# A graph network's attention rounds with edges on partitions instead of features

## Chip, cores and metric

One core of one Trainium2 chip. The metric is the device time of one launch in microseconds: 8402.46 us, median of three runs (8401.58 to 8409.89).

## What is computed

A stack of four graph layers over 3125 nodes and 103125 edges sorted by target node, with 64 features; each layer is added to its input and normalised. In the kernel they are seven rounds over the edges: one sum, two attention rounds, one relation-typed sum, three maxima. The attention rounds are these:

```
e = edge_attr @ we                                # 32 attributes per edge
ke = k[src] + e
score = sum(q[dst] * ke, axis=-1) / sqrt(64)
a = exp(score - segment_max(score, dst)[dst])
alpha = a / segment_sum(a, dst)[dst]
out = segment_sum(alpha[:, None] * (v[src] + e), dst) + x @ ws + bs
```

The products with `wk`, `wv` and `we` are taken out of the edges: an edge's row is [x of source (64), attributes (32), 1], 97 wide (`KA`); the query of a target node is projected onto those 97 columns beforehand, and the weighted row sums are multiplied by the value weights afterwards, per node.

## The kernel before, in words

Edges are padded to 202 chunks (`C`) of 512 (`EC`), each of four tiles (`TC`) of 128 edges. Every round is one software pipeline over its chunks, and each engine has its own instruction stream, written by `chunks(eng, steps, (lag, stage), ...)`: in step t it calls the stages in the order in which they are listed, each with chunk t minus its lag. Within an engine's stream nothing overtakes; between engines the stages wait for counters, and `wait(...)` names the counter and the chunk. Small buffers are rings: `U` = 4 slots for data that DMA brings, `V` = 2 for products on the chip and for the PSUM banks.

In an attention round a chunk goes this way. ACT copies the chunk's source indices (`indices`, L845); POOL gathers the source rows with one indirect DMA for each tile (L799), edges on partitions. SP fetches flags, one-hot tile, four windows of the query table and the attributes, which are stored with features on rows (`fetch`, from L713). PE turns the gathered rows so that features lie on partitions (`turn`, L948) and multiplies windows with one-hots to give each edge the query of its target (`query`, three bf16 parts for each tile, L973). DVE multiplies both (`product`, L1129). PE sums over features with a matrix of constants, which puts the score on all 97 rows (`score`, L981). DVE forms the running maximum (scan, L1152), two differences and the decay (L1156, L1159, L1161), ACT takes two exponentials (L870, L872), DVE weights the row (L1134) and sums it with a scan (L1095), whose factor drops to zero where a new target begins. PE turns the result back (`back`, L995), ACT copies and stores it (L864, L891). At the end of a round POOL gathers each node's last row (L809), and node-wise work follows.

The stage orders of the attention rounds are `(0, turn), (0, query), (1, score), (3, back)` on PE (L1001) and `(0, product), (2, accumulate), (1, maxima)` on DVE (L1165). The sum round also makes the one-hot tiles (L1102) that later rounds read. The relation round is a gather, a weighting on DVE (L1113), `turn`, scan and `back`.

## Time and profile before

| | |
|---|---|
| median of the runs | 8402.46 us |
| profiled execution, its own time | 8402.05 us |
| its span | 8400.2 us |
| busy: POOL, PE, DVE, ACT | 5613.3, 4720.2, 3677.3, 2039.9 us |
| gathers of source rows | 5656, 957 ns each |
| mean granted TensorE clock | 0.634 |
| DMA | 896.47 MB, mean 107 GB/s |

### The profile page before, as it was taken

To read this page: it belongs to the slowest core of one execution; us is meant where nothing else is said; L and a number is where in the kernel's file an instruction comes from. 1 tells how busy PE (TensorE), PEld (TensorE's weight loads), DVE (VectorE), ACT (ScalarE), POOL (GpSimd) and SP (SyncE) were. 2 spreads that over 40 slices of the span, in tenths; PEclk is the share of its full clock that TensorE was granted. 3 is DMA by queue.
4 is the path that set the end of the run, shared out by engine and by line. 5 is a ranking of instruction groups with operands and counts; after the bars stand their busy time and mean duration, and the time that the engine had idled before them with its cause. 6 is when DMAs were issued, how large, how long until landed. Compare 5 with 4: busy or idle time off the path is not lost.

```text
span 8400.2 us, 120802 instructions
## 1 busy us (share of the span) xinstructions
PE 4720.2 (56%) x23315; PEld 2797.9 (33%) x23315; DVE 3677.3 (44%) x5268; ACT 2039.9 (24%) x4886; POOL 5613.3 (67%) x5874
## 2 busy tenths in 40 slices
PE   2333347777766777776533333666646666566664
PEld 1222234444444444444222222333323333233332
DVE  5444459999967999994133332111111111111112
ACT  1111124444433444442111111111111111111111
POOL 6777756666645666662477775777767777677776
PEclk9999985555555555555555555555556656556555
DMA  4444446665645666662322223444434444444443
GB/s 127 121 127 122 124 92 129 129 130 129 130 96 115 130 130 130 130 130 45 95 59 59 59 59 74 112 112 112 112 88 112 112 112 112 89 108 112 112 112 86
DMA packets 1878056, 896.47 MB, mean 107 GB/s; under 512 B 1293716, under 2 KB 1754724, under 8 KB 1871588
## 3 DMA queue, kind: packets, MB, share of 16 engines
q1 hardware_dynamic: 769476, 429.40, 20.4%
q10 hardware_dynamic: 921120, 272.38, 14.1%
q0 software_dynamic: 187392, 193.93, 12.9%
q8 instruction: 25, 0.41, 0.0%
q14 instruction: 43, 0.35, 0.0%
HBM read 642.32 MB, written 252.51 MB: 107 GB/s over the span
## 4 chain that ended last, share of the span: by engine, by line
PE 23%; issue 18%; POOL 8%; DMA 3%; DVE 2%; ACT 1%; POOLq 0%; DVEq 0%; ACTq 0%
POOL rows L799 8%; PE ps L987 6%; PE ps L962 6%; PE ps L958 5%; DMA rows<-src_table,idx 2%; PE ps L995 2%; PE ps L512 1%; PE ps L563 1%; PE ps L948 1%; PE ps L505 0%; DVE rows L1113 0%; POOL agg L809 0%; DMA agg<-states_sum,last_i 0%; DMA states_sum<-hb 0%; DVE agg L618 0%
## 5 line engine op out<-in xcount | busy, mean ns | idle before, releaser
L799 POOL DMA_INDIRECT rows<-src_table,idx x5656 | 5411.7, 957 | 2553.3 <-issue 1590.2
L948 PE MATMUL ps<-ident,rows 128*64 128x128 f32 x3232 | 839.1, 414 | 1432.3 <-DVE rows L1113 672.6
L1095 DVE TENSOR_TENSOR_SCAN st<-pen,st,ps 128x512 f32<-128x512 f32 x300 | 383.8, 1279 | 2592.3 <-PE ps L987 2592.2
L958 PE MATMUL ps<-ident,rows 128*128 128x128 f32 x1212 | 563.0, 464 | 1173.8 <-issue 1025.6
L995 PEld LDWEIGHTS ps<-ident,st 64*128 64x128 f32 (+2 forms) x4444 | 689.5, 211 | 1269.6 <-issue 1226.5
L995 PE MATMUL ps<-ident,st 64*128 64x64 f32 (+2 forms) x4444 | 905.7, 355 | 242.1 <-issue 216.3
L948 PEld LDWEIGHTS ps<-ident,rows 128*64 128x64 f32 x3232 | 478.4, 164 | 1570.3 <-issue 1394.1
L981 PE MATMUL ps<-prod,eighth 97*97 97x512 f32 x808 | 681.9, 940 | 453.3 <-issue 430.5
L1095 DVE TENSOR_TENSOR_SCAN st<-xe,st,ps 64x512 f32<-64x512 fp8e4 x402 | 511.1, 1271 | 876.2 <-issue 457.7
L958 PEld LDWEIGHTS ps<-ident,rows 128*128 128x128 f32 x1212 | 219.2, 181 | 1430.2 <-issue 1268.4
L882 ACT ACTIVATE xe<-ps,b 128x512 f32<-128x512 f32 x303 | 208.2, 687 | 1916.9 <-PE ps L962 1916.9
L962 PE MATMUL ps<-sel,win 128*64 128x128 fp8e4 x7272 | 647.6, 313 | 0.0
L987 PE MATMUL ps<-xe,w 128*128 128x512 f32 x606 | 625.3, 1135 | 0.0
L856 ACT ACTIVATE pen<-sel 97x512 f32<-97x512 fp8e4 x404 | 254.4, 630 | 1474.1 <-DVE decay L1159 1474.1
L973 PEld LDWEIGHTS ps<-sel,win 128*97 128x97 bf16 x4848 | 586.3, 203 | 17.0
L973 PE MATMUL ps<-sel,win 128*97 128x128 fp8e4 x4848 | 586.4, 309 | 0.0
L1095 DVE TENSOR_TENSOR_SCAN st<-decay,st,msg 97x512 f32<-97x512 f32 x402 | 516.4, 1285 | 132.6 <-DVE msg L1134 131.7
L864 ACT ACTIVATE hb<-ps 128x256 f32<-128x256 f32 (+1 forms) x808 | 346.1, 428 | 762.8 <-PE ps L995 762.7
L1152 DVE TENSOR_TENSOR_SCAN runmax<-pen,runmax,ps 97x512 f32<-97x512 f32 x404 | 512.4, 1268 | 20.2 <-issue 2.2
L962 PEld LDWEIGHTS ps<-sel,win 128*64 128x64 bf16 x7272 | 357.3, 152 | 267.6 <-issue 263.5
L981 PEld LDWEIGHTS ps<-prod,eighth 97*97 97x97 f32 x808 | 142.1, 230 | 520.4 <-issue 505.5
L862 ACT ACTIVATE hb<-ps 128x512 f32<-128x512 f32 x303 | 180.9, 597 | 552.7 <-PE ps L995 520.8
(150 smaller groups left out, 4061.8 us busy)
## 6 DMA issues: line engine op xcount, KB each, us to landing
states_sum<-hb ACTq DMA_DIRECT2D x1010, 128.0 KB
win<-dst_table SPq DMA_DIRECT2D x1616, 72.8 KB
rows<-src_table,idx POOLq DMA_INDIRECT x5656, 2.4
states_att<-hb ACTq DMA_DIRECT2D x404, 194.0 KB
win<-dst_table ACTq DMA_DIRECT2D x1212, 48.0 KB
win<-dst_table SPq DMA_DIRECT2D x1212, 48.0 KB
dst_b<-in_dst_row SPq DMA_DIRECT2D x50, 1024.0 KB
sel<-onehots SPq DMA_DIRECT2D x303, 128.0 KB
```

The costliest lines, as they stand in the source:

```text
L799: pool.indirect_dma_start(rows[:, s, j * D:(j + 1) * D], None, srcs[q.r], bass.IndirectOffsetOnAxis(ap=idx[:, s, j:j + 1], axis=0))\
L856: nc.scalar.activation(pen[0:kw, s % V, :], sel[0:kw, s, EC:2 * EC], ACT.Copy, scale=BIG, bias=-BIG)\
L864: nc.scalar.activation(hb[:, s, 0:TC * kw], bank(BACK, s)[:, 0:TC * kw], ACT.Copy)\
L948: last = nc.tensor.matmul(bank(TURNED, s)[0:D, j * P:(j + 1) * P], rows[:, s, j * D:(j + 1) * D], ident[:, :], is_transpose=True, start=Tr ...
L958: nc.tensor.matmul(bank(TURNED, s)[:, at_j], rows[:, s, j * P:(j + 1) * P], ident[:, :], is_transpose=True, start=True, stop=False)
L962: last = nc.tensor.matmul(bank(TURNED, s)[h * D:h * D + D, at_j], win_pair(s, j, h)[:, i * D:(i + 1) * D], sel[:, s, h * EC + j * P:h * EC ...
L973: last = nc.tensor.matmul(bank(QUERY, s)[0:KA, j * P:(j + 1) * P], win_att(s, j)[:, i * KA:(i + 1) * KA], sel[:, s, j * P:(j + 1) * P], st ...
L981: nc.tensor.matmul(bank(SCORE, s)[0:KA, :], eighth[0:KA, 0:KA], prod[:, s % V, :], start=True, stop=True).then_inc(q.score_ready.sem, 1)
L987: nc.tensor.matmul(bank(QUERY, s), w2[:, q.r - 4, :], xe[:, s, :], start=True, stop=True).then_inc(q.lifted.sem, 1)
L995: last = nc.tensor.matmul(bank(BACK, s)[:, j * w:(j + 1) * w], st[0:w, s % V, j * P:(j + 1) * P], ident[0:w, 0:w], is_transpose=True, star ...
L1095: nc.vector.tensor_tensor_scan(st[0:w, s % V, :], d0, d1, init, op0, op1).then_inc(q.st_ready.sem, 1)
L1152: nc.vector.tensor_tensor_scan(m, pen[0:KA, s % V, :], bank(SCORE, s)[0:KA, :], before[:, 0:1], ALU.add, ALU.max).then_inc(q.max_ready.sem, 1)
```

## The change

All in the two attention rounds, with preparations ahead of them. Edges stay on partitions until the weighted rows are made:

- The edge attributes are turned once, in the sum round, into a table `edge_rows` with one row of 128 B for each edge (`fetch_edges`, `turn_edges`, `edges_back`, `store_edges`). In an attention round SP fetches them straight behind the 64 gathered features, into rows of 97 (`xe_a`). The ring of these rows has 8 slots (`UA`).
- `turn` and the large `score` product are gone. `query` has its operands swapped, so that the query comes out with edges on partitions. `product` multiplies 128x388 and a reduction over 97 columns gives one score for each edge, 4 columns a chunk.
- The softmax is done for groups of four chunks (`GC`), 16 tiles (`GT`): one transpose puts 16 tiles on 16 partitions (`turn_scores`), two scans of 128 columns, forward and backward, give each segment's maximum within the tile (`segments`), the maxima of the tiles' ends go through a scan on one partition (`turn_ends`, `running`, `turn_run`), then come the difference, the exponential and the turn back (`differences`, `weights`, `turn_weights`). Penalties for these scans are made at the start and kept in `pens` and `row_pen`.
- `weigh` multiplies the rows by their weights, `turn_weighted` turns them, one scan sums them as before (`accumulate`). Its factor is the flag, and at each tile's first edge the carried factor of `kept` (`decays`).

The core of the diff; `LW` is 5:

```diff
+UA = 2 * 4
+GC = UA // 2
+GT = GC * TC
+NG = -(-C // GC)
+NS = 2
+LW = GC + 1
+B = 4
+PF = 2 * P + 1
...
+        xe_a = edges_a[:, 0:UA * TC * KA].rearrange("p (u f) -> p u f", u=UA)
...
+                def gather_att(c, s, n):
+
+                    wait(pool, *sources_stored(q), (q.idx_ready, c + 1), (q.weighted, c - UA + 1))
+                    for j in range(TC):
+                        pool.indirect_dma_start(xe_a[:, s, j * KA:j * KA + D], None, srcs[q.r],
+                                                bass.IndirectOffsetOnAxis(ap=idx_a[:, s, j:j + 1], axis=0))\
+                            .then_inc(q.rows_ready[s].sem, 16)
...
+                def weights(c, s, n):
+
+                    if not group(c, s, n):
+                        return
+                    g, gs_, m = group(c, s, n)
+                    wait(act, (q.diff_ready, g + 1))
+                    nc.scalar.activation(weight_t[0:m, :], weight_t[0:m, :], ACT.Exp, scale=float(D) ** -0.5)\
+                        .then_inc(q.weight_ready.sem, 1)
+                    wait(act, (q.weight_turned, g + 1), (q.weighted, GC * (g - NS + 1)))
+                    nc.scalar.activation(weight[:, gs_, 0:m], weight_ps[:, 0:m], ACT.Copy).then_inc(q.weight_out.sem, 1)
...
-                    chunks(act, q.steps, (U, features), (0, indices), (U, penalty), (U + 2, exponentials),
-                           (U + 3, states_out), (U + 4, store_states))
+                    chunks(act, q.steps, (B + 2, kept), (B + 2, weights), (B + LW, decays), (0, indices_att),
+                           (B + LW + 2, states_out), (B + LW + 3, store_states), ring=UA)
...
-                    wait(pe, (q.in_ready[s], 16 * (TC + 2) * (n + 1)), (q.prod_ready, c - V + 1))
+                    v = s % U
+                    wait(pe, (q.in_ready[v], 16 * (TC + 1) * (n * (UA // U) + s // U + 1)), (q.prod_ready, c - V + 1))
                     for j in range(TC):
                         for i in range(3):
-                            last = nc.tensor.matmul(bank(QUERY, s)[0:KA, j * P:(j + 1) * P],
-                                                    win_att(s, j)[:, i * KA:(i + 1) * KA],
-                                                    sel[:, s, j * P:(j + 1) * P], start=i == 0, stop=i == 2)
+                            last = nc.tensor.matmul(bank(TURNED, s)[:, j * KA:(j + 1) * KA], sel[:, v, j * P:(j + 1) * P],
+                                                    win_att(v, j)[:, i * KA:(i + 1) * KA], start=i == 0, stop=i == 2)
                     last.then_inc(q.query_ready.sem, 1)
...
-                def score(c, s, n):
-
-                    wait(pe, (q.prod_ready, c + 1), (q.diff_ready, c - V + 1))
-                    nc.tensor.matmul(bank(SCORE, s)[0:KA, :], eighth[0:KA, 0:KA], prod[:, s % V, :],
-                                     start=True, stop=True).then_inc(q.score_ready.sem, 1)
+                def turn_scores(c, s, n):
+
+                    if not group(c, s, n):
+                        return
+                    g, gs_, m = group(c, s, n)
+                    wait(pe, (q.scored, c + 1), (q.diff_ready, g))
+                    nc.tensor.matmul(score_t[0:m, :], score[:, gs_, 0:m], ident[:, :], is_transpose=True,
+                                     start=True, stop=True).then_inc(q.score_turned.sem, 1)
+
+                def turn_ends(c, s, n):
+
+                    if not group(c, s, n):
+                        return
+                    g, gs_, m = group(c, s, n)
+                    wait(pe, (q.seg_ready, g + 1), (q.run_ready, 4 * g))
+                    for o, e in ((first_ps, 0), (last_ps, P - 1)):
+                        last = nc.tensor.matmul(o[:, 0:m], seg_max[0:m, e:e + 1], ident[0:m, 0:m],
+                                                is_transpose=True, start=True, stop=True)
+                    last.then_inc(q.ends_turned.sem, 1)
+
+                def turn_run(c, s, n):
+
+                    if not group(c, s, n):
+                        return
+                    g, gs_, m = group(c, s, n)
+                    wait(pe, (q.run_ready, 4 * g + 3), (q.ref_ready, g))
+                    nc.tensor.matmul(run_t[0:m, :], run_in[:, 0:m], ident[0:1, 0:1], is_transpose=True,
+                                     start=True, stop=True).then_inc(q.run_turned.sem, 1)
+                    wait(pe, (q.kept_ready, g + 1), (q.weight_out, g))
+                    nc.tensor.matmul(kept_ps[:, 0:m], ones_row[:, :], kept_row[:, 0:m],
+                                     start=True, stop=True).then_inc(q.kept_spread.sem, 1)
+
+                def turn_weights(c, s, n):
+
+                    if not group(c, s, n):
+                        return
+                    g, gs_, m = group(c, s, n)
+                    wait(pe, (q.weight_ready, g + 1), (q.kept_out, g + 1))
+                    nc.tensor.matmul(weight_ps[:, 0:m], weight_t[0:m, :], ident[0:m, 0:m],
+                                     is_transpose=True, start=True, stop=True).then_inc(q.weight_turned.sem, 1)
+
+                def turn_weighted(c, s, n):
+
+                    wait(pe, (q.weighted, c + 1), (q.st_ready, c - V + 1))
+                    for j in range(TC):
+                        last = nc.tensor.matmul(bank(QUERY, s)[0:KA, j * P:(j + 1) * P],
+                                                weighted[:, s % V, j * KA:(j + 1) * KA], ident[:, :],
+                                                is_transpose=True, start=True, stop=True)
+                    last.then_inc(q.turned.sem, 1)
...
-                    chunks(pe, q.steps, (0, turn), (0, query), (1, score), (3, back))
+                    chunks(pe, q.steps, (1, turn_scores), (2, turn_run), (2, turn_weights), (0, query), (1, turn_ends),
+                           (LW, turn_weighted), (LW + 1, back), ring=UA)
...
+                    wait(dve, (q.query_ready, c + 1), (q.rows_ready[s], 16 * TC * (n + 1)), (q.edge_ready[s], 16 * (n + 1)),
+                         (q.scored, c))
+                    nc.vector.tensor_tensor(prod[:, :], bank(TURNED, s)[:, 0:TC * KA], xe_a[:, s, :], ALU.mult)\
                         .then_inc(q.prod_ready.sem, 1)
+                    wait(dve, (q.prod_ready, c + 1))
+                    o = (s % GC) * TC
+                    nc.vector.reduce_sum(score[:, s // GC, o:o + TC], prod[:, :].rearrange("p (j f) -> p j f", f=KA),
+                                         axis=AX.X).then_inc(q.scored.sem, 1)
+
+                def segments(c, s, n):
+
+                    if not group(c, s, n):
+                        return
+                    g, gs_, m = group(c, s, n)
+                    wait(dve, (q.score_turned, g + 1), (q.pens_ready[gs_], 16 * (n + 1)), (q.seg_ready, g))
+                    nc.vector.tensor_tensor_scan(tile_max[0:m, :], pens_sb[0:m, gs_, P:2 * P], score_t[0:m, :], -BIG,
+                                                 ALU.add, ALU.max).then_inc(q.scanned.sem, 1)
+                    wait(dve, (q.scanned, g + 1), (q.ref_ready, g))
+                    nc.vector.tensor_tensor_scan(seg_max[0:m, ::-1], pens_sb[0:m, gs_, 2 * P:P:-1], tile_max[0:m, ::-1],
+                                                 -BIG, ALU.add, ALU.max).then_inc(q.seg_ready.sem, 1)
+
+                def running(c, s, n):
+
+                    if not group(c, s, n):
+                        return
+                    g, gs_, m = group(c, s, n)
+                    o = gs_ * GT
+                    wait(dve, (q.ends_turned, g + 1), (q.row_pens_ready, g + 1), (q.run_ready, 4 * g), (q.run_turned, g),
+                         (q.kept_ready, g))
+                    if gs_ == 0 and not (isinstance(c, int) and c < GC):
+                        nc.vector.tensor_copy(run[:, 0:1], run[:, NS * GT:NS * GT + 1]).then_inc(q.run_carried.sem, 1)
+                        wait(dve, (q.run_carried, n))
+                    init = run[:, o:o + 1]
+                    nc.vector.tensor_tensor_scan(run[:, 1 + o:1 + o + m], row_pens[:, gs_, 0, 0:m], last_ps[:, 0:m],
+                                                 init, ALU.add, ALU.max).then_inc(q.run_ready.sem, 1)
...
+                    wait(dve, (q.run_ready, 4 * g + 3))
+                    nc.vector.tensor_tensor(run_diff[:, 0:m], run_in[:, 0:m], run_ref[:, 0:m], ALU.subtract)\
+                        .then_inc(q.run_ready.sem, 1)
+
+                def differences(c, s, n):
+
+                    if not group(c, s, n):
+                        return
+                    g, gs_, m = group(c, s, n)
+                    wait(dve, (q.run_turned, g + 1), (q.diff_ready, g))
+                    nc.vector.scalar_tensor_tensor(ref[0:m, :], pens_sb[0:m, gs_, 0:P], run_t[0:m, :], seg_max[0:m, :],
+                                                   ALU.add, ALU.max).then_inc(q.ref_ready.sem, 1)
+                    wait(dve, (q.ref_ready, g + 1), (q.weight_turned, g))
+                    nc.vector.tensor_tensor(weight_t[0:m, :], score_t[0:m, :], ref[0:m, :], ALU.subtract)\
+                        .then_inc(q.diff_ready.sem, 1)
+
+                def weigh(c, s, n):
+
+                    gs_, o = s // GC, (s % GC) * TC
+                    of = lambda rows_of: rows_of.rearrange("p (j f) -> p j f", f=KA)
+                    wait(dve, (q.weight_out, n * NS + gs_ + 1), (q.turned, c - V + 1))
+                    nc.vector.tensor_tensor(of(weighted[:, s % V, :]), of(xe_a[:, s, :]),
+                                            weight[:, gs_, o:o + TC].unsqueeze(2).to_broadcast([P, TC, KA]), ALU.mult)\
+                        .then_inc(q.weighted.sem, 1)
 
                 def accumulate(c, s, n):
-                    wait(dve, (q.exp_ready, c + 1), (q.xe_ready, c + 1))
-                    nc.vector.tensor_tensor(msg[:, s % V, :], diff[:, s % V, :], xe[0:KA, s, :], ALU.mult)\
-                        .then_inc(q.msg_ready.sem, 1)
-                    wait(dve, (q.decay_ready, c + 1), (q.msg_ready, c + 1))
-                    scan(c, s, decay[:, s % V, :], msg[:, s % V, :], ALU.mult, ALU.add)
-
...
+
+                    wait(dve, (q.turned, c + 1), (q.decay_ready, 2 * (c + 1)))
+                    scan(c, s, decay[:, s % V, :], bank(QUERY, s)[0:KA, :], ALU.mult, ALU.add)
...
-                    chunks(dve, q.steps, (0, product), (2, accumulate), (1, maxima))
+                    chunks(dve, q.steps, (2, differences), (0, product), (1, segments), (LW + 1, accumulate), (LW, weigh),
+                           (1, running), ring=UA)
```

## Rows read from the trace of the kernel before

**Rows 1.** the page's busy time of each engine over the whole span

```profile
PE 4720.2 (56%) x23315; PEld 2797.9 (33%) x23315; DVE 3677.3 (44%) x5268; ACT 2039.9 (24%) x4886; POOL 5613.3 (67%) x5874
```

**Rows 2.** windows: first line names columns; sum, attention, relation round

```profile
core 0: us, PE busy (x) PEld busy (x) DVE busy (x) ACT busy (x) POOL busy (x), PEclk, DMA share, GB/s
600.00:900.00 300.00, 99.06 (x480) 62.22 (x480) 123.29 (x300) 47.20 (x179) 227.19 (x240) 1.00 0.47 124
1500.00:1800.00 300.00, 216.66 (x1039) 140.73 (x1038) 271.76 (x354) 124.09 (x282) 185.94 (x189) 0.60 0.61 129
4500.00:4800.00 300.00, 99.03 (x480) 62.15 (x480) 101.90 (x120) 35.35 (x120) 226.85 (x241) 0.50 0.29 59
```

**Rows 3.** groups, attention round, 1500 to 2100 us: gathers and product

```profile
L799 POOL DMA_INDIRECT rows<-src_table,idx x378 | 372.7, 986 | 230.0 <-ACT idx L845 137.0 <-issue 93.0
...
L1129 DVE TENSOR_TENSOR prod<-ps,xe 97x512 f32<-97x512 f32 x94 | 64.4, 685 | 0.9
```

**Rows 4.** timeline, attention round: start us, duration us, engine, line, what

```profile
1802.39 0.68 DVE L1129 TENSOR_TENSOR prod<-ps,xe 97x512 f32<-97x512 f32 x1
...
1803.03 0.69 DVE L1134 TENSOR_TENSOR msg<-diff,xe 97x512 f32<-97x512 f32 x1
...
1804.04 1.28 DVE L1095 TENSOR_TENSOR_SCAN st<-decay,st,msg 97x512 f32<-97x512 f32 x1 [0.32 <-DVE msg L1134]
...
1805.43 0.88 PE L995 MATMUL ps<-ident,st 97*128 97x97 f32 x4 [0.26 <-issue]
...
1806.10 1.06 PE L948 MATMUL ps<-ident,rows 128*64 128x128 f32 x4
...
1806.96 1.49 PE L973 MATMUL ps<-sel,win 128*97 128x128 fp8e4 x12
...
1808.59 0.68 DVE L1129 TENSOR_TENSOR prod<-ps,xe 97x512 f32<-97x512 f32 x1
```

**Rows 5.** timeline: first product, first gather of results, first attention round

```profile
1166.88 0.69 DVE L1129 TENSOR_TENSOR prod<-ps,xe 97x512 f32<-97x512 f32 x1 [9.50 <-PE ps L973]
...
2465.65 0.94 POOL L809 DMA_INDIRECT agg<-states_att,last_i  x1 [43.91 <-DMA states_att<-hb]
```

**Rows 6.** groups of the whole span, shapes near to those of the change

```profile
L602 DVE TENSOR_TENSOR agg<-agg,ga 128x388 f32<-128x388 f32 x12 | 6.8, 565 | 0.4
...
L386 DVE TENSOR_TENSOR split_r<-ps,split 128x388 f32<-128x388 f32 x12 | 6.7, 561 | 90.4 <-ACT split L375 90.4
...
L1035 DVE TENSOR_REDUCE within<-agg 128x4 f32<-128x512 f32 x6 | 4.1, 686 | 0.2
...
L1067 DVE TENSOR_TENSOR tile_same<-pen,split 40x128 fp8e4<-40x128 int32 x1 | 0.3, 277 | 0.0
...
L1036 DVE SCALAR_TENSOR_TENSOR edges_le<-tiles_le,within 128x1 f32<-128x1 f32 x1 | 0.2, 158 | 0.0
...
L444 ACT ACTIVATE rT<-ps 97x128 f32<-97x128 f32 x2 | 0.5, 268 | 1.6 <-PE ps L505 1.6
```

**Rows 7.** timeline, relation round: weighting, turning, scan

```profile
4501.30 0.43 DVE L1113 TENSOR_TENSOR rows<-rows,wgt_sb 128x256 f32<-128x256 f32 x1 [3.06 <-DMA rows<-src_table,idx]
...
4501.98 1.03 PE L948 MATMUL ps<-ident,rows 128*64 128x128 f32 x4 [4.48 <-DVE rows L1113]
...
4503.11 1.27 DVE L1095 TENSOR_TENSOR_SCAN st<-xe,st,ps 64x512 f32<-64x512 fp8e4 x1 [1.38 <-PE ps L948]
```

**Rows 8.** timeline of PE where the granted clock first changes

```profile
1174.86 1.06 PE L948 MATMUL ps<-ident,rows 128*64 128x128 f32 x4 [0.32 <-DMA rows<-src_table,idx]
...
1179.98 0.62 PE L948 MATMUL ps<-ident,rows 128*64 128x128 f32 x4 [1.08 <-DMA rows<-src_table,idx]
1180.44 0.83 PE L973 MATMUL ps<-sel,win 128*97 128x128 fp8e4 x12
...
1182.02 0.55 PE L995 MATMUL ps<-ident,st 97*128 97x97 f32 x4
```

**Rows 9.** timeline: the sum round's first onehots

```profile
66.89 0.87 DVE L1102 TENSOR_SCALAR sel<-dst_b,nodes 128x128 fp8e4<-128x128 int32 x4 [8.24 <-DMA xe<-flags]
```

More of the change, by code:

```diff
@@ L66, in gnn_kernel @@
     onehots = dram("onehots", (C, P, EC), u8)
+    pens = dram("pens", (T, PF), f32)
+    edge_rows = dram("edge_rows", (EP, DE), f32)
     flags = dram("flags", (C, EC), u8)
@@ L179, in gnn_kernel @@
         flags_stored = sem("flags_stored")
+        pens_made = sem("pens_made")
+        pens_stored = sem("pens_stored")
+        rows_set = sem("rows_set")
+        ids_turned = sem("ids_turned")
+        ones_set = sem("ones_set")
+        edge_loaded = [sem(f"edge_loaded{s}") for s in range(U)]
+        edge_stored = [sem(f"edge_stored{s}") for s in range(U)]
+        edge_turned = sem("edge_turned")
+        edge_copied = sem("edge_copied")
         out_stored = sem("out_stored")
@@ L252, in __init__ @@
+                if kind == MAX:
+                    self.in_ready = [shared(f"in_ready_{s_}", 16 * (2 * TC + 3) * len(range(s_, C_, U))) for s_ in range(U)]
                 uses = [(C_ - s_ + U - 1) // U for s_ in range(U)]
@@ L254, in __init__ @@
                 self.st_stored = [shared(f"st_stored_{s_}", 16 * self.per_step * uses[s_]) for s_ in range(U)]
-                if kind == ATT:
-                    self.edge_ready = [shared(f"edge_ready_{s_}", 16 * uses[s_]) for s_ in range(U)]
                 self.src_stored = [sem(f"src_stored_{r}_{s_}") for s_ in range(V if kind == REL else 1)]
@@ L800, in gather @@
                                                 bass.IndirectOffsetOnAxis(ap=idx[:, s, j:j + 1], axis=0))\
-                            .then_inc(q.rows_ready[s], 16)
-                chunks(pool, q.steps, (0, gather))
+                            .then_inc(q.rows_ready[s].sem, 16)
[4 more added lines that the diff above has]
+                                                bass.IndirectOffsetOnAxis(ap=idx_a[:, s, j:j + 1], axis=0))\
+                            .then_inc(q.rows_ready[s].sem, 16)
+                if q.kind == ATT:
+                    chunks(pool, q.steps, (0, gather_att), ring=UA)
+                else:
+                    chunks(pool, q.steps, (0, gather))
                 kw = KA if q.kind == ATT else D
@@ L917, in _ @@
                 else:
-                    chunks(act, q.steps, (0, indices), (U + 1, states_out), (U + 2, store_states))
+                    chunks(act, q.steps, (0, indices), *[(U, edges_back)] * (k == SUM), (U + 1, states_out),
+                           (U + 2, store_states))
                 node_act(act, q)
@@ L937, in _ @@
                 .then_inc(pe_pre, 1)
+            pe.wait_ge(rows_set, 1)
+            for b in range(TB):
+                w = min(P, T - b * P)
+                last = nc.tensor.matmul(last_ids[:, b * P:b * P + w], tile_last[0:w, b:b + 1], ident[0:w, 0:w],
+                                        is_transpose=True, start=True, stop=True)
+            last.then_inc(ids_turned, 1)
             for q in rounds:
@@ L1004, in _ @@
                 else:
-                    chunks(pe, q.steps, (0, turn), (1, back))
+                    chunks(pe, q.steps, *[(0, turn_edges)] * (k == SUM), (0, turn), (1, back))
                 if k == MAX:
```

302 lines of the change are left out of this document (208 added, 94 removed).

## Prediction

> **What bounds the kernel now.** I read the page first: POOL is busy for 67% of the span, more than any other engine [rows 1]. A share of the whole span hides the stages, so next come windows, one per kind of round [rows 2]. In the sum round and in the relation round POOL issues 240 gathers in 300 us, that is 1.25 us each or 5.0 us a chunk of four tiles, and nothing else is near its limit. In the attention round (1500 to 1800 us) POOL falls to 189 gathers while DVE is busy 271.8 of 300 us: there DVE is the bound. The groups of 1500 to 2100 us say the same from both ends [rows 3]: the gathers idle 137.0 us for the indices, which come free only as DVE moves on, and `product` runs 94 times in 600 us, 6.38 us a chunk. The timeline shows why a wait inside that loop costs nothing today [rows 4]: PE's stream of `back`, `turn` and `query` starts at 1805.43 and its last product ends at 1808.45, while DVE goes through its seven passes; PE is about one step ahead. From the first product of the first attention round to the first gather of its results is 2465.65 - 1166.88 = 1298.8 us [rows 5], so 202 chunks of 6.36 us and 14 us of ends. The two attention rounds have 404 chunks. The sum is made against the profiled execution, 8402.05 us (span 8400.2 us), which stands at the median of 8402.46 us.
>
> **What the change takes from DVE.** Of the old seven passes five go: `diff`, two for `decay`, `msg` and the running maximum's 512 columns; `product` is kept with another shape. Per chunk now: product 128x388 from PSUM 0.56, row sum of 388 columns 0.56 (a reduction of 512 columns, 0.686, costs what a tensor-tensor of 512 does, 0.685, so 388 columns as well go by the 388 rows), weighting 0.565, scan 1.285 [rows 3, 4, 6]. With one wait on itself between product and sum (0.10, between the 0.32 of the `msg` to scan gap and nothing) and 0.08 of overlap for each of two passes that follow without a dependence (1802.39 + 0.68 against 1803.03 shows about that) this is 2.90 us [rows 4]. If DVE alone counted, the gathers' 5.0 us would be the bound and each round would lose about 270 us.
>
> **Why I don't count that gain: the order of the two queues.** In step t PE's order is turn_scores, turn_run, turn_weights, query(t), turn_ends, turn_weighted(t-5), back(t-6). DVE's is differences, product(t), segments, accumulate(t-6), weigh(t-5), running. turn_weighted(t-5) waits for weigh(t-5), which stands behind product and scan of the same step; query(t+1) stands behind it on PE; and product(t+1), the first pass of DVE's next step, waits for query(t+1). So the engines take turns, DVE idle while PE works and the other way round. One plain step is this ring:
> - DVE, product to end of weigh: 2.90.
> - DVE to PE: 0.25; weighting ends at 4501.73 and PE's transposes start at 4501.98 [rows 7].
> - turn_weighted, four f32 transposes with 128 moving columns: 0.85, the distance from `turn` to `query` (1806.96 - 1806.10, rounded) [rows 4].
> - back(t-6): 0.67, 1806.10 - 1805.43 [rows 4].
> - query, 12 products: 1.49 to the end of the last as it is now [rows 4]. The stationary side is now the one-hot tile with 128 columns and the moving side has 97 instead of 128. 0.67 to 0.85 is 97 to 128, so f32 transposes go by moving columns; by that the query would be 1.18. I take 1.25 and keep 1.18 to 1.49.
> - PE to DVE: 0.10 in the relation round (PE's modelled end to scan) [rows 7]; `product` has three more waits behind the first, and the 0.32 gap is the far end [rows 4]. I take 0.20.
>
> Sum 2.90 + 0.25 + 0.85 + 0.67 + 1.25 + 0.20 = 6.12 us, against 6.36 now. Halving DVE's work gains almost nothing per plain step.
>
> The Trainium skill, page "TensorE: Matmul & The Clock Gate", section "Weight-path perf modes", says that non-f32 weights of exactly 128 columns are loaded by a faster path; by it the query would be at its 1.18 and the sum 0.07 lower per chunk. No row of before has such weights in fp8, so the trace doesn't show it.
>
> **What a group of four chunks adds to the ring.**
> - Step after the group's last product: one transpose of scores ahead of query, 0.21 (a quarter of 0.85). Two scans over 16x128 on DVE ahead of weigh: no row has one; bounds are a quarter of 1.285, 0.32, and 0.16 (one-element pass) plus a quarter of the rest, 0.44 [rows 4, 6]. I take 0.40 each, with a self-wait: 0.90.
> - `running` (a one-partition scan and three tiny passes at 0.16 [rows 6] with self-waits, about 1.1) runs while PE does turn_weighted and back (1.77), so it is covered; without that cover it would cost 1.1 a group.
> - Next step: PE turns the running row (0.25, estimate from the tails above), DVE does two passes over 16x128 (0.28 each, the 40x128 row [rows 6], with waits 0.75), ACT takes the exponential (0.27, the 97x128 row [rows 6], plus 0.1), PE turns the weights (0.25 with the handoff), and only then query(t) and product(t). That is 1.6. ACT's own order can add to it (copy of the penalties, states_out, the carried factor's exponential and copy stand before it): I take 1.75, between 1.3 and 2.8.
> - Together 2.86, or 0.72 a chunk; from 0.55 to 1.05.
>
> So 6.12 + 0.72 = 6.84 us a chunk against 6.36.
>
> **The clock is a term of this.** PE's part of the ring is priced at the half level. In the attention round the granted clock is 0.60, in the relation round 0.50 [rows 2], where four transposes take 1.03 [rows 7]. In the sum round the record reads 1.00 [rows 2] and at 1174.86 four still take 1.06; from 1179.98 they take 0.62 and the query 0.83 [rows 8], so the record before its first change says nothing and only the durations count: half level (1.2 GHz) in the sum and relation rounds, mostly half in the attention round, full (2.4 GHz) for stretches of it. In the changed round PE works in two short runs a step with DVE's passes between them, which is more like the relation round than today's attention round. I take the half level. A mean of 0.60 as now would take some 0.2 a chunk off.
>
> **The rest.** The first five steps of a round have no weigh and no scan and are paced by gathers (5.0): -9. The drain is six steps of scan, weigh, handoff, turn (some 3.1 each) and a group's chain, 22, and landing of the last store, 4. A round from first product is 202 x 6.84 - 9 + 26 = 1399, against 1299: +100, twice. POOL (5.0), ACT (about 1.8) and SP stay below 6.84 in work, the buffers of eight chunks put gathers two steps ahead, so the smaller pieces of the attributes' rows (128 B) fall on no path by their time of 0.61 x 6.36 = 3.9 us of DMA a chunk today [rows 2]. In the sum round four transposes, a copy, a load and a store a chunk lie beside 5.0 us of gathers: PE is busy 99 of 300 us there [rows 2]; SP's new wait for the copy has only batches of onehots behind it, wanted two chunks later. I take +2, 0 to 20. At the start some 11 us of new DVE passes and SP's wait for the first of them stand before the first onehots, where DVE idles 8.24 us now [rows 9]; four chunks of gathers (20 us) cover it: +3, 0 to 8.
>
> The Trainium skill, page "DMA: Bandwidth & Descriptors", section "Specifications", puts line rate at pieces of 512 B and more, which speaks against 512 pieces of 128 B a chunk where 32 of 2 KB were. As an estimate by it: were each charged as 512 B, 256 KB at the 129 GB/s of the attention round [rows 2] are 2 us where 64 KB are 0.5, so 3.9 becomes 5.4 us a chunk. That is under 6.84, so the sum stays; it would put a floor of 5.4 in place of 5.0 under the second rival, 8035 instead of 7870. No row of before has such pieces.
>
> 8402 + 200 + 5 = 8607, say 8605 us.
>
> **Rivals.**
> - Full clock in the ring: PE's 2.77 falls to about 1.65 (0.46 + 0.36 + 0.83 [rows 8]) and a group's chain by 0.3. Step 5.0 + 0.6 = 5.6, a round 1147 from the first product, 8100 us. For it: the full level does occur now. Against: in the relation round, where PE also rests between short runs, no row is at that level. It decides from a mean clock of about 0.75 up. Chance 0.09.
> - It does what it should: the queues run apart, gathers bound at 5.0, a round of 1030: 7870 us. It would need query(t+1) issued before turn_weighted(t-5), which the order of the stages excludes. 0.04.
> - The chain of a group is far longer (ACT's order, each wait between small passes at 0.32): 1.3 a chunk and 6.4 plain, 7.7: 8950 us. Speaks for it: eleven small handoffs; against: the covers above. 0.09.
> - Short terms throughout (plain 5.9, group 0.5, 6.4): no change, 8425 us. This side also ends in a gain if the mean clock stays at 0.60: 8350. 0.08.
> - The forecast, 8450 to 8800: 0.70.
>
> The range 8380 to 8850 leaves out the first three rivals, about 0.2. About 0.2% (17 us) is what a measurement of this kernel can tell from no change. Faster by more: 0.09 + 0.04 + 0.04 = 0.17. Within: 0.04. Slower: 0.79.
>
> **What would show it.** Right: in the attention rounds DVE's idle time ahead of `product` is put to PE's query, about 3 us a chunk; PE's idle ahead of turn_weighted is put to DVE's weighting; gathers idle for the weighting; DVE is busy about 3.5 of 6.8 us; one step in four shows a PE gap before query that ends with ACT's exponential; the clock is near 0.5. Wrong: gathers at 1.25 us apiece there, a clock well over 0.6, or DVE going from weigh straight to the next product.

## The result, and the profile after

The changed kernel takes 8517.65 us (median of 4, 8514.4 to 8528.23), the kernel before beside it 8402.68 us (8401.58 to 8409.89): ratio 1.0137, 95% interval 1.0121 to 1.0153. It is slower, by 115 us. The prediction said slower, and put the loss 87 us too high (8605 us).

The profiled execution took 8528.23 us (span 8526.3 us). First the page's busy line and three windows of it (sum, attention and relation round; columns as in [rows 2]):

```profile
PE 4234.0 (50%) x24036; PEld 2816.2 (33%) x24036; DVE 2692.1 (32%) x4738; ACT 1622.4 (19%) x4790; POOL 5780.2 (68%) x5874
```

```profile
600.00:900.00 300.00, 132.25 (x720) 92.16 (x720) 122.89 (x296) 58.83 (x239) 227.35 (x239) 1.00 0.60 150
1500.00:1800.00 300.00, 141.21 (x994) 125.80 (x992) 148.34 (x276) 68.00 (x235) 197.79 (x183) 1.00 0.59 123
4500.00:4800.00 300.00, 99.07 (x480) 62.25 (x480) 101.64 (x119) 35.15 (x119) 227.14 (x240) 1.00 0.29 59
```

Against [rows 1] DVE lost 985 us of work and the span still grew. Against [rows 2] the sum round (239 gathers for 240) and the relation round are as they were. In the attention round DVE's work falls from 271.8 to 148.3 of 300 us, yet POOL issues 183 gathers where it issued 189: no engine is full any more, and the round is slower. That is the picture of engines that take turns. The DMA engines' share is 0.59 of this window for 0.61, some 3.9 us a chunk both times, so the attributes' pieces of 128 B cost nothing that can be seen.

By the first gather of each round's results, the sum round's is 7.5 us later than before (1092.61 for 1085.08), the first attention round adds 51.8, the second 59.8, and all that follows 7: 126 us in the profiled executions. The end of the first attention round, for the second of [rows 5], and its first product, for the first:

```profile
1173.37 0.56 DVE L1364 TENSOR_TENSOR prod<-ps,edges_a 128x388 f32<-128x388 f32 x1 [8.43 <-PE ps L1138]
...
2524.95 0.94 POOL L927 DMA_INDIRECT agg<-states_att,last_i  x1 [39.81 <-DMA states_att<-hb]
```

1351.6 us, for 1298.8. The waits of 1500 to 2100 us (engine, what waited, for whom: us in total, times, longest) and the timeline of one whole ring:

```profile
PE ps L1187 <- issue: 222.8, 79, 3.1
ACT decay L1022 <- DVE st L1331: 184.2, 67, 3.0
...
DVE prod L1364 <- issue: 156.1, 55, 3.0
...
POOL edges_a L913 <- DVE weighted L1424: 102.6, 41, 3.3
DVE prod L1364 <- PE ps L1138: 102.6, 36, 3.2
```

```profile
1808.00 0.56 DVE L1364 TENSOR_TENSOR prod<-ps,edges_a 128x388 f32<-128x388 f32 x1 [2.21 <-PE ps L1138]
1808.66 0.56 DVE L1368 TENSOR_REDUCE score<-prod 128x4 f32<-128x388 f32 x1
1809.14 1.27 DVE L1331 TENSOR_TENSOR_SCAN st<-decay,st,ps 97x512 f32<-97x512 f32 x1
1810.33 0.54 DVE L1424 TENSOR_TENSOR weighted<-edges_a,weight 128x388 f32<-128x388 f32 x1
...
1810.96 1.14 PE L1187 MATMUL ps<-ident,weighted 128*97 128x128 f32 x4 [3.06 <-issue]
...
1811.90 0.85 PE L1203 MATMUL ps<-ident,st 97*128 97x97 f32 x4
...
1812.55 1.19 PE L1138 MATMUL ps<-win_sb,sel 128*128 128x97 bf16 x12
...
1813.83 0.56 DVE L1364 TENSOR_TENSOR prod<-ps,edges_a 128x388 f32<-128x388 f32 x1 [2.96 <-issue]
```

Follow it round: DVE works from 1808.00 to 1810.87 while PE sits idle for 3.06 us. PE's three groups run from 1810.96 to 1813.74 while DVE sits idle for 2.96 us. Then DVE's next product starts, 5.83 us after the last one. Neither engine is waiting for data from outside; each waits for the other. ("issue" means that the profile names nobody who ended the wait; the starts and ends show the partner.)

### The profile page after: what moved, and what is told of

Read it like the earlier page. It is cut to its first block, busy times and chain, and to the rows that moved or that the text cites. A ratio compares the mean times of both kernels' runs of the same rounds, so it can differ in the third digit from the quotient of the medians.

```text
span 8526.3 us, 122130 instructions
## 1 busy us (share of the span) xinstructions
PE 4234.0 (50%) x24036; PEld 2816.2 (33%) x24036; DVE 2692.1 (32%) x4738; ACT 1622.4 (19%) x4790; POOL 5780.2 (68%) x5874
## 4 chain that ended last, share of the span: by engine, by line
PE 23%; issue 17%; POOL 8%; DMA 3%; DVE 2%; ACT 1%; POOLq 0%; ACTq 0%; DVEq 0%
POOL edges_a L906 8%; PE ps L1195 6%; PE ps L1126 6%; PE ps L1122 5%; DMA edges_a<-src_table,idx 3%; PE ps L1203 2%; PE ps L584 1%; PE ps L635 1%; PE ps L1112 1%; PE ps L577 0%; DVE edges_a L1349 0%; POOL agg L927 0%; PE ps L1187 0%; DMA agg<-states_sum,last_i 0%; DMA states_sum<-hb 0%
## 5 line engine op out<-in xcount | busy, mean ns | idle before, releaser
L906 POOL DMA_INDIRECT edges_a<-src_table,idx x4040 | 3832.2, 949 | 1519.6 <-issue 1162.6
L913 POOL DMA_INDIRECT edges_a<-src_table,idx x1616 | 1747.0, 1081 | 998.2 <-issue 459.9
L1122 PE MATMUL ps<-ident,edges_a 128*128 128x128 f32 x1212 | 562.5, 464 | 1176.9 <-issue 1029.2
L1112 PE MATMUL ps<-ident,edges_a 128*64 128x128 f32 x1616 | 418.9, 415 | 1259.9 <-DVE edges_a L1349 674.1
L1187 PE MATMUL ps<-ident,weighted 128*97 128x128 f32 x1616 | 462.2, 441 | 1061.3 <-issue 915.6
L1331 DVE TENSOR_TENSOR_SCAN st<-edges_a,st,ps 64x512 f32<-64x512 fp8e4 x402 | 511.3, 1272 | 878.1 <-issue 483.5
L1126 PE MATMUL ps<-sel,win_sb 128*64 128x128 fp8e4 x7272 | 647.3, 313 | 0.0
L1195 PE MATMUL ps<-edges_a,w 128*128 128x512 f32 x606 | 627.1, 1138 | 0.0
L1331 DVE TENSOR_TENSOR_SCAN st<-decay,st,ps 97x512 f32<-97x512 f32 x402 | 511.7, 1273 | 10.5 <-PE ps L1187 10.1
L1138 PE MATMUL ps<-win_sb,sel 128*128 128x97 bf16 x4848 | 476.5, 283 | 32.4 <-DMA win_sb<-dst_table 32.4
L1138 PEld LDWEIGHTS ps<-win_sb,sel 128*128 128x128 fp8e4 x4848 | 432.9, 144 | 48.9 <-DMA win_sb<-dst_table 34.3
```

Of the source, the lines that this page charges most:

```text
L906: pool.indirect_dma_start(rows[:, s, j * D:(j + 1) * D], None, srcs[q.r], bass.IndirectOffsetOnAxis(ap=idx[:, s, j:j + 1], axis=0))\
L913: pool.indirect_dma_start(xe_a[:, s, j * KA:j * KA + D], None, srcs[q.r], bass.IndirectOffsetOnAxis(ap=idx_a[:, s, j:j + 1], axis=0))\
L1112: last = nc.tensor.matmul(bank(TURNED, s)[0:D, j * P:(j + 1) * P], rows[:, s, j * D:(j + 1) * D], ident[:, :], is_transpose=True, start=Tr ...
L1122: nc.tensor.matmul(bank(TURNED, s)[:, at_j], rows[:, s, j * P:(j + 1) * P], ident[:, :], is_transpose=True, start=True, stop=False)
L1126: last = nc.tensor.matmul(bank(TURNED, s)[h * D:h * D + D, at_j], win_pair(s, j, h)[:, i * D:(i + 1) * D], sel[:, s, h * EC + j * P:h * EC ...
L1138: last = nc.tensor.matmul(bank(TURNED, s)[:, j * KA:(j + 1) * KA], sel[:, v, j * P:(j + 1) * P], win_att(v, j)[:, i * KA:(i + 1) * KA], st ...
```

## The experiments

The profile alone can't say what the order of PE's queue costs, nor what comes next once that order is gone. The theory had two halves: the ring sets the plain steps, and it does so only because turn_weighted(t-5) stands ahead of query(t+1) behind a wait for DVE. Take the order away and the product intervals must fall to what DVE needs. The rivals: the ring is only a picture and something else (a group's chain, SP, the gathers) holds the round; or the ring is real and one of these lies close behind it.

One thing has to be said for all of them: the four chips these twelve runs were made on are slower with this program than the first. The kernel before takes 9627 to 9862 us there. So each run is held against the kernel before on its own chip, and against the changed kernel repeated on one of them (g1_changed). In their sum rounds POOL issues about 200 gathers in 300 us where the first chip had 240, and in stretches SP spends some 0.7 us on one register or issue instruction. No trace of the kernel before exists from those chips, so how much of its own extra time lies in which round is not known.

The figure I read in each trace is the time from one `product` to the next, as medians by the chunk's place in its group of four, with the mean. The first value is the step from a group's first product to its second: the softmax of the 16 tiles of the group before stands in it, and I call it the step behind a group. All are worked out from the start times of the 9th to the 202nd product of the first attention round:

| kernel | intervals, us | mean, us | ratio to before |
|---|---|---|---|
| before (first chip) | 6.20 6.57 6.28 6.44 | 6.37 | 1 |
| changed (first chip) | 8.82 5.83 5.82 6.04 | 6.62 | 1.0137 |
| g1_changed | 10.38 6.50 5.83 6.79 | 7.36 | 1.0334 |
| e2_query_first | 11.07 6.55 5.83 6.11 | 7.45 | 1.0317 |
| e1_apart | 15.48 3.99 4.75 6.15 | 7.80 | 1.0459 |
| e3_both | 15.10 3.96 4.47 7.23 | 7.71 | 1.0417 |
| e4_query_third | 13.79 5.17 5.94 5.89 | 8.09 | 1.0528 |
| g2_near128 | 10.33 6.51 7.22 6.47 | 7.69 | 1.0449 |
| g3_both_near128 | 14.90 3.58 3.17 7.23 | 7.11 | 1.0196 |
| g4_both_near_each | 13.11 4.28 4.97 6.26 | 7.08 | 1.0217 |
| h1_one_gather | 7.12 4.74 3.07 4.02 | 4.81 | 0.9219 |

**1. PE's order.** Three edits of one list, the third being both of the others:

```diff
 # e1_apart
-  (LW, turn_weighted), (LW + 1, back), ring=UA)
+  (LW + 1, turn_weighted), (LW + 2, back), ring=UA)
 # e2_query_first
-  chunks(pe, q.steps, (1, turn_scores), (2, turn_run), (2, turn_weights), (0, query), (1, turn_ends),
+  chunks(pe, q.steps, (0, query), (1, turn_scores), (2, turn_run), (2, turn_weights), (1, turn_ends),
```

> Changed kernel with one edit: PE's turn_weighted and back run one step later (lags 6 and 7 instead of 5 and 6), so query(t+1) no longer stands behind the weighting of DVE's step t. Theory A (PE and DVE take turns, a ring of 5.8 us a plain step): plain steps fall to the gathers' 5.0 us, the group's chain is still ahead of one query in four; 5.0 to 5.5 us a chunk, 7870 to 8100 us, most likely 7950. Theory B (supply of data, that is gathers of 1.08 us and their landing, or the DMA engines, sets the 6.6 us a chunk): no change, 8500 to 8530 us.

> Changed kernel with another single edit: on PE query(t) is the first stage of a step, ahead of turn_scores, turn_run and turn_weights; turn_weighted and back stay where they are. A: the ring of 5.8 us stays, the group's part (3.1 us per four chunks, of which some 1.8 us stand ahead of query) shrinks: 6.1 to 6.3 us a chunk, 8320 to 8400 us. B: no change, 8500 to 8530 us.

> Both edits of the two runs before. A: neither the ring nor the group's chain holds a query back, so the gathers' 5.0 us a chunk are the bound: 7850 to 7900 us, DVE busy under 4 of 5 us. B: no change. A third possibility, that DMA with its 128 B pieces has a floor above 5.0 us a chunk, would show here as 5.2 to 5.6 us a chunk, 7950 to 8110 us, with long gaps until rows or windows land.

Measured: e1_apart 10294.41 us, 1.0459 (1.0429 to 1.0489); e2_query_first 10163.84, 1.0317 (1.0287 to 1.0348); e3_both 10249.45, 1.0417 (1.0384 to 1.045); before 9852.46. The ring is confirmed and the gain is not: all three times lie outside what either theory gave. With e1's order the first plain step falls to 3.99 us (the next two are 4.75 and 6.15) and the two engines overlap, as its timeline shows (query starts while DVE weights, turn_weighted while DVE multiplies):

```profile
1805.16 0.54 DVE L1424 TENSOR_TENSOR weighted<-edges_a,weight 128x388 f32<-128x388 f32 x1
...
1805.29 1.14 PE L1138 MATMUL ps<-win_sb,sel 128*128 128x97 bf16 x12 [0.97 <-issue]
...
1806.22 1.13 PE L1187 MATMUL ps<-ident,weighted 128*97 128x128 f32 x4
...
1806.52 0.56 DVE L1364 TENSOR_TENSOR prod<-ps,edges_a 128x388 f32<-128x388 f32 x1 [0.82 <-PE ps L1138]
```

But the step behind a group takes 15.48 us, and the mean is 7.80 us a chunk, no shorter than the 7.36 of g1_changed on another chip. The query first alone changes nothing in plain steps, since it still stands behind the turn_weighted of the step before. Nor does it shorten the step behind a group, 11.07 us for 10.38, as I had expected it to. PE's query no longer stands behind the softmax, but `differences` still stands ahead of `product` on DVE and waits for PE's `turn_run`: its `ref` (L1413) waits 5.54 us there (median), against 1.07 in g1.

**2. A shorter query.** The two lower bf16 parts of the node values are left out of the query, 4 products in place of 12 (so the scores are coarser):

```diff
-  for i in range(3):
-      last = nc.tensor.matmul(..., win_att(v, j)[:, i * KA:(i + 1) * KA], start=i == 0, stop=i == 2)
+  last = nc.tensor.matmul(..., win_att(v, j)[:, 0:KA], start=True, stop=True)
```

> Changed kernel, but the query is made from only the highest of its three bf16 parts, 4 products a chunk instead of 12 (the two lower parts of the query are left out); the same data are still fetched. A: eight products of 0.081 us fewer in the ring, -0.65 us a chunk, 8255 us (8230 to 8290). B: no change, 8500 to 8530 us.

Measured: 10366.38 us, 1.0528 (1.0497 to 1.0559). The first plain step is 5.17 us, 0.66 less than the undisturbed 5.83 of the changed kernel on the first chip, and the query's group is 0.53 where it was 1.19: what is taken from PE's part of a step comes off the step one for one, as a ring demands. (Its third and fourth intervals don't show it; on the next chip they do, 5.21 and 5.39.) The forecast of 8255 us for theory A is missed all the same: the time again goes to the step behind a group, 13.79 us.

**3. The same three on another chip**, to see whether the long step belongs to one chip (before 9691.7 us there).

> The same kernel as e1_apart, whose call ran on a chip on which every round, the untouched ones too, was some 17% longer (the kernel before 9852 us, every engine standing still for up to 12 us at a time with nothing released). If this chip runs the kernel before in about 8402 us: A (ring): 7870 to 8100 us, most likely 7950. B (data supply): 8500 to 8530 us. If this chip is like that one, stalls of issue hide both.

> The same kernel as e3_both. If the kernel before takes about 8402 us: A: gathers' 5.0 us a chunk, 7850 to 7900 us. B: no change, 8500 to 8530 us. Floor of DMA: 7950 to 8110 us.

> The same kernel as e4_query_third (the two lower parts of the query are left out). If the kernel before takes about 8402 us: A: 8255 us (8230 to 8290). B: 8500 to 8530 us.

Measured: 1.042 (1.0381 to 1.0459), 1.0396 (1.0352 to 1.044), 1.043 (1.0386 to 1.0475), with steps behind a group of 14.57, 14.37 and 13.72 us. The long step doesn't belong to one chip. In f3_both SP's queue waits for nothing between 1800 and 2400 us, so I took SP for the next bound. Its queue has one odd entry, there already in the changed kernel on the first chip (start, duration):

```profile
1811.81 0.29 SPq L804 DMA_DIRECT2D sel<-flags  x1
...
1812.41 8.46 SPq L816 DMA_DIRECT2D sel<-onehots  x1
...
1821.64 1.88 SPq L822 DMA_DIRECT2D win_sb<-dst_table  x4
```

The issue that follows the fetch of the near flags (4 x 512 bytes a partition to 97 partitions, 194 KB, once in four chunks; the "4 x 128" of g2's expectation should be this) holds SP for 8.46 us; others of that line take 0.34.

**4. The fetch behind which SP stands.** g1_changed is the changed kernel. g2_near128 fetches the flags to 128 partitions, g3_both_near128 does this and both orders of PE, g4_both_near_each has both orders and fetches each chunk's flags alone, as the kernel before does.

```diff
 # g2, g3
-  sp.dma_start(sel[0:KA, 0:m, ...], flags[of, :]. ... .to_broadcast([KA, m, EC]))
+  sp.dma_start(sel[:, 0:m, ...], flags[of, :]. ... .to_broadcast([P, m, EC]))
 # g4, for every chunk
+  sp.dma_start(sel[:, s % U, ...], flags[one(c)].to_broadcast([P, EC]))
```

> The changed kernel itself, as the anchor of the three beside it on the same chip. Both theories: its time stands to the kernel before as in the first comparison, ratio 1.010 to 1.045 (the upper part of that if this chip's SP takes as long per issue as in the first two sets of runs).

> Only the fetch of the near flags is widened from 97 to 128 partitions, once per four chunks. Theory 'shape' (SP is blocked 8.4 us behind that fetch because it goes to 97 partitions): the block falls below 1 us, SP's 24.6 us per group of four to about 17; the ring sets the plain steps as before (5.83 us), so on a chip where the ring is the bound the time stays within 0.5% of the changed kernel, and where SP is the bound the group step (8.8 us and more) falls by up to the 8 us. Rival 'bytes' (it is the 4 x 128 flags on so many partitions at one go): the block stays 8.3 us or grows with 128/97 to 11 us, and the time is unchanged or up to 2% longer.

> Both changes of TensorE's order (turn_weighted and back one and two chunks later, the query first) with the fetch over 128 partitions. Theory 'ring, then SP, by shape': plain steps near 3.9 us, group step no longer 14 to 15 but 8 to 9 us, mean 5.0 to 5.3 us per chunk, ratio to the kernel before 0.93 to 0.96. Rival 'bytes': group step stays at 14 to 15, ratio 1.02 to 1.05 as with the fetch over 97.

> The same two changes of order, with the near flags fetched for each chunk alone, 128 x 512 bytes, as the kernel before does (where the issue behind it takes 0.34 us). Both theories expect the 8.4 us block to be gone: group step 8 to 9 us, plain steps near 4 to 4.5, mean 5.0 to 5.5 per chunk, ratio to the kernel before 0.93 to 0.97. If it stays at 1.02 to 1.05, SP's block is not what the freed ring runs into.

Measured, with 9646.42 us for the kernel before: g1 9965.48 us, 1.0334 (1.0317 to 1.0351); g2 10074.97, 1.0449 (1.0432 to 1.0466); g3 9835.93, 1.0196 (1.0177 to 1.0215); g4 9846.59, 1.0217 (1.02 to 1.0234). The odd entry is the shape's doing. In g2 it is gone:

```profile
1840.81 0.38 SPq L804 DMA_DIRECT2D sel<-flags  x1
1841.43 0.35 SPq L816 DMA_DIRECT2D sel<-onehots  x1
```

Over the whole execution the mean of L816 falls from 2293 ns (g1) to 306. And it was worth nothing by itself: g2 is slower than g1 by 1.1%, which I can't explain (its third interval is 1.4 us longer). With the ring apart it seems to help: g3 against f3_both, 1.0196 for 1.0396, but these ran on two chips. The pair that tests the order of the stages alone, on one chip, is g2 and g3. With both edits of PE's list the time falls from 10074.97 to 9835.93 us, 2.4%, and the mean from 7.69 to 7.11 us a chunk: the ring did cost time. But my 0.93 to 0.96 for g3 and 0.93 to 0.97 for g4 were wrong. The step behind a group stays at 13 to 15 us, so SP's block was not what the freed ring runs into. POOL's groups (1800 to 2400 us) of the changed kernel on the first chip and of g3 suggested what was left:

```profile
L913 POOL DMA_INDIRECT edges_a<-src_table,idx x362 | 393.2, 1086 | 208.2 <-DVE weighted L1424 105.8 <-issue 102.3
```

```profile
L913 POOL DMA_INDIRECT edges_a<-src_table,idx x339 | 363.4, 1072 | 237.2 <-DVE weighted L1424 137.8 <-issue 99.4
```

In g3 16 gathers at 1.07 us and 0.30 between two are 22 us, and 137.8 us of waiting over 600 us are 6.5 us in each group of 28.4: POOL either gathers or is held. In the changed kernel on the first chip it is about 22 and 4.7 of 26.5. POOL stands still while the softmax of 16 tiles holds back the weighting, because the buffers of gathered rows come free only with it. Then it gathers without a break, and, by the reading I went on with, the step behind a group waits for it. The next kernel takes gathers away.

The trace of g3 itself doesn't bear this reading out for the step behind a group. Here is one such step, which ends with the product of 1808.21:

```profile
1799.45 7.81 SPq L822 DMA_DIRECT2D win_sb<-dst_table  x4
...
1800.97 0.47 PE L1171 MATMUL ps<-kept_row,ones_row 1*97 1x16 f32 x2 [1.43 <-ACT kept_row L1001]
...
1804.48 0.94 POOL L913 DMA_INDIRECT edges_a<-src_table,idx  x1 [0.30 <-issue]
...
1807.48 0.34 DVE L1413 SCALAR_TENSOR_TENSOR ref<-pens_sb,ps,seg_max 16x128 f32<-16x128 f32 x1 [7.92 <-remote]
1807.52 0.18 ACT L1004 ACTIVATE kept_part<-ps 97x16 f32<-97x16 f32 x1 [6.65 <-remote]
...
1808.21 0.56 DVE L1364 TENSOR_TENSOR prod<-ps,edges_a 128x388 f32<-128x388 f32 x1
```

DVE stands still ahead of `ref`, not ahead of `product`, which follows without a pause. `ref` waits for PE's `turn_run`, whose transpose the trace ends at 1799.55, and the gathers of this product's chunk had been issued long before: over the round, their last issue ends 13.2 us (median, 8.5 at least) ahead of the second product of a group. DVE, ACT and SP start again together at about 1807.5, and until then SP's single instructions take 0.7 us. Over the round `ref` starts 7.8 us (median) behind PE's transpose. So the step behind a group is not held by rows that are missing. Only ahead of a group's first product are the gathers close: it starts 3.4 us (median) behind the end of its last gather's issue.

**5. Fewer gathers.** g3 with one gather a chunk instead of four; the other three tiles are read by one plain transfer from fixed rows (those tiles' sources are left out of the computation), with the waits matched to it, same bytes.

```diff
-  for j in range(TC):
+  for j in range(1):
       pool.indirect_dma_start(xe_a[:, s, j * KA:j * KA + D], None, srcs[q.r], ...)
+  pool.dma_start(xe_a[:, s, KA:TC * KA]. ... [:, :, 0:D], srcs[q.r][0:P * (TC - 1), :]. ...)
```

> The kernel with both changes of TensorE's order and the fetch over 128 partitions, in which POOL gathers one tile per chunk through its list of sources; the other three tiles of a chunk are read by one plain transfer from fixed rows, so their features are not those of the edges' sources (that part of the computation is left out). POOL's 16 gathers per four chunks (about 1.07 us and 0.3 us between two, 22 us) become 4 and 4 plain issues. Theory 'gathers and their buffers': once the ring is apart, the group step waits for gathers that start only when the weighted rows have freed a buffer (POOL waited 6.3 us per group for them, then gathered without a pause); group step falls from 15 to 8 to 9 us, mean from 7.1 to 5.0 to 5.5 us per chunk, ratio to the kernel before 0.93 to 0.96. Rival 'supply and chain': the group step is held by the stretches in which SP takes 0.7 us per instruction and the other engines start nothing, and by the group's own chain; it stays 13 to 15 us, mean 6.6 to 7.2, ratio 1.00 to 1.03.

Measured: 8896.78 us against 9656.68 on its chip, 0.9219 (0.919 to 0.9248): below even the 0.93 of what "gathers and their buffers" gave. The step behind a group falls from 14.9 to 7.12 us and the mean from 7.11 to 4.81. So the gathers, or something that comes only with them, hold g3. POOL's two groups of 1800 to 2400 us, and DVE's waits ahead of `ref` in g3 and then in h1:

```profile
L913 POOL DMA_INDIRECT edges_a<-src_table,idx x106 | 106.1, 1001 | 323.1 <-DVE weighted L1427 297.3 <-issue 25.8
L916 POOL DMA_DIRECT2D edges_a<-src_table x106 | 84.1, 793 | 0.0
```

```profile
L1413 DVE SCALAR_TENSOR_TENSOR ref<-pens_sb,ps,seg_max 16x128 f32<-16x128 f32 x21 | 7.2, 345 | 146.0 <-remote 145.9
```

```profile
L1416 DVE SCALAR_TENSOR_TENSOR ref<-pens_sb,ps,seg_max 16x128 f32<-16x128 f32 (+1 forms) x28 | 9.6, 344 | 1.9
```

Of the 9.2 us a group between the two kernels, 6.9 are the wait ahead of `ref` (146.0/21 less 1.9/28) and some 3 the wait ahead of `product` (89.7/21 less 36.6/28). The first is nearly all that the step behind a group loses (14.9 less 7.12 is 7.8 by the medians), and in g3 it was no wait for rows. The rival, "stretches in which SP takes 0.7 us per instruction", is therefore not excluded: h1 took these stretches away too. SP's instructions of 0.6 to 0.85 us add up to 243 of the 1200 us from 1400 us in g3 and to 14 in h1, and in g3's first attention round 210 of 284 us of them lie in steps behind a group. That dense gathers bring them about is likely by h1 and not shown. And the granted clock in the window of 1800 to 2400 us is 0.62 instead of 0.56, with more groups of four transposes at 0.65 us, the full level, beside others at 1.14. The shares of these in the 2.3 us a chunk are not told apart.

## Why the prediction was right, and where it was off

**The bound before.** Held: once DVE's passes were nearly halved, DVE's work was no longer what set the round, and nothing else was full.

**The plain ring, forecast 6.12, measured 5.83.** Term by term, from the ring above: DVE 2.90, measured 2.87. turn_weighted 0.85, 0.94 from its start to that of back. back 0.67, 0.65. query 1.25, 1.19. The handoffs are what was mis-sized: DVE to PE 0.25, measured 0.09; PE to DVE 0.20, measured 0.09. I took the first from the relation round's 0.25 and set the second above its 0.10 for the number of waits ahead of `product`; waits that are already met cost nothing to see here. These two are 0.27 of the 0.29 us. That the other terms come out within 0.09 with errors of both signs is partly luck.

The query's 1.19 is the value that moving columns give (1.18). The Trainium skill, "TensorE: Matmul & The Clock Gate", section "Weight-path perf modes", names a faster weight load for 128-column non-f32 weights. The prediction's value by it was the same 1.18, so the measured 1.19 agrees with it and doesn't show whether it was at work.

**The group's addition, forecast 2.86, measured about 3.2** (8.82 - 5.83 in the step behind a group, and 0.21 in the step before it). The two scans over 16x128 take 0.40 and 0.41, as taken. The chain through ACT and back is what was mis-sized:

```profile
1804.03 0.85 PE L1203 MATMUL ps<-ident,st 97*128 97x97 f32 x4
...
1806.15 0.31 ACT L1012 ACTIVATE weight_t<-weight_t 16x128 f32<-16x128 f32 x1
...
1806.75 1.16 PE L1138 MATMUL ps<-win_sb,sel 128*128 128x97 bf16 x12
```

The query starts 2.72 us behind the start of `back`, where it is 0.65 in a plain step: 2.07 for 1.75. This term was too small by 0.3 a group, 0.08 a chunk. So 5.83 + 0.80 = 6.63 a chunk, for 6.84, and 6.62 is what the products show.

**Ends and other rounds.** 202 x 6.62 = 1337 of the 1351.6 us: 14 for the ends, forecast 17. Sum round and start +7.5, forecast 5. The forecast of +100 a round came out at +52 and +60; 202 x (6.84 - 6.62) = 44 is nearly all of the difference, and 0.29 of the plain ring less 0.08 of the group makes it up.

**The clock.** Half level was right (the 1174.86 of [rows 8] that I put in the sum round lies in the first attention round; the argument stands without it). The record misleads again as in [rows 8]: it reads 1.00 in the attention round (0.846 over the span), but every whole group of four transposes there takes 1.14 us, the half level. The 0.65 of g3 and h1 is what they take at the full one. Read by the record alone, a named sign of being wrong ("a clock well over 0.6") and the mark of the first rival ("a mean clock of about 0.75 up") would both have been there; the durations set them aside.

**The signs named beforehand.** DVE idle ahead of `product` 2.96 us, PE idle ahead of turn_weighted 3.06, gathers idle for the weighting 102.6 of 600 us, DVE 148.3 of 300 us (3.3 of 6.6 a chunk), one step in four longer, with PE idle ahead of turn_weights until ACT's exponential: all there, the clock by durations only.

**The rivals.** "It does what it should, 5.0 us a chunk": excluded as written, since e1 shows that this needs another order. But its price was wrong. I took 5.0 from the sum round's gathers, where the buffer of a chunk comes free steadily. In the attention round the gathers take more, 1.39 us apiece with the 0.30 between two, 5.5 a chunk; and with the order mended a chunk takes 7.1 us on a slower chip. Likewise "the buffers of eight chunks put gathers two steps ahead" holds while the ring paces them: a group's first product starts 8.2 us (median) behind its last gather's issue in the changed kernel and 3.4 in g3. That error didn't touch the forecast; it would have spoiled any advice drawn from it. Full clock in the ring didn't occur.

What stays open: what the mended order would bring on the first chip, where SP had no slow stretches in its attention rounds; g3 was not run there. Open is also what holds PE's signals and SP back for some 8 us in the steps behind a group of g3. Of the kernels that leave nothing out, none is faster than the kernel before on its own chip.

## What to carry to other kernels

Before counting work taken off a busy engine as time, write the two engines' queues for step t side by side: if A's first wait in a step is for B's last item, and B's last item stands behind a wait for A, the step costs the sum of both, however small each is. A wait one step later in one queue takes the ring apart, but look first for how close the next bound lies: here a gather engine needs 5.5 of the step's 6.6 us (four times 1.09 + 0.30), and the softmax done in batches of four holds it back once in four steps. Take the suspected next bound away in one kernel (as h1 does) before building on a fix, and look at which instruction the wait stands ahead of: an engine that gathers without a break is not yet the one that the others wait for.

## What the runs showed that I had not expected

- A broadcast of 4 x 512 bytes to 97 partitions holds SP's next issue for about 8.4 us (median of 100 in the changed kernel, 8.0 to 10.5; 8.8 in f3_both); the same to 128 partitions, or one chunk's flags at a time, does not (0.33 us). In the changed kernel it cost nothing that shows: g2, without it, is no faster than g1.
- Chips differ in this program by up to 17% for the same kernel (8402 to 9862 us). In the traces of the slow ones SP's simple instructions take 0.7 us in stretches. In the attention rounds these went with dense gathers (243 of the 1200 us from 1400 us in g3, 14 in h1); that one causes the other is not shown.
- A plain transfer on POOL's queue is not free: 793 ns for three tiles, against 1001 ns for a gather of one.
